# Softmax exponentials head by head on ScalarE, with the maximum as bias and the sum as a by-product

## The reference, cut to what matters

```
h = max(layernorm(x), 0)
x = x + L0(h, adj, adj, b)            # A = adj h, C = adj h + b; maximum over nodes of relu
h = max(layernorm(x), 0)              # (of layer 1)
q, k, v = h Wq + bq, h Wk + bk, h Wv + bv        # 8 heads of 64
scores  = q k^T / 8 + (adj == 0 ? -1e9 : 0)
weights = softmax(scores)             # over the keys, for each head and row
out     = x + weights v
```

## Time and profile before

| what | value |
|---|---|
| time, median of 3 runs | 1316.65 us (1316.41 to 1317.42) |
| the profiled execution's own time | 1314.74 us |
| its span, first to last instruction | 1313.0 us |
| TensorE busy | 1283.2 us, 98% |
| VectorE busy | 1056.3 us, 80% |
| ScalarE busy | 945.6 us, 72% |
| GpSimd busy | 1028.8 us, 78% |
| granted TensorE clock, mean | 0.994 of full |

### The profile page before, as it was taken

How to read it: one execution, slowest core, us unless ns; L and a number is a source line. 1 busy time by engine, 2 the same in 40 slices (tenths; PEclk the granted TensorE clock), 3 DMA queues, 4 the chain that set the end, 5 groups by cost and what they waited for, 6 DMA issues and landing times.

```text
span 1313.0 us, 30866 instructions
## 1 busy us (share of the span) xinstructions
PE 1283.2 (98%) x11193; PEld 670.7 (51%) x11193; DVE 1056.3 (80%) x2217; ACT 945.6 (72%) x1451; POOL 1028.8 (78%) x1165
## 2 busy tenths in 40 slices
PE   6999999999999999999999999999999999999995
PEld 3455555555555555555555555555555555555553
DVE  7588788788788888888888888887887887888777
ACT  6877777777777777777777777777777777777665
POOL 5887877887887888788788778778778778878665
PEclk9999999999999999999999999999999999999998
DMA  6366566566555555555555655655665665664344
GB/s 201 67 137 137 123 143 133 127 138 136 130 132 142 131 124 145 135 121 146 137 122 138 139 127 134 137 133 127 139 137 121 141 142 121 136 144 116 89 89 112
DMA packets 435237, 171.68 MB, mean 131 GB/s; under 512 B 400528, under 2 KB 400656, under 8 KB 435088
## 3 DMA queue, kind: packets, MB, share of 16 engines
q1 hardware_dynamic: 433744, 169.46, 56.2%
q10 hardware_dynamic: 1344, 0.27, 0.1%
HBM read 37.03 MB, written 33.55 MB: 54 GB/s over the span
## 4 chain that ended last, share of the span: by engine, by line
PE 94%; DVE 3%; ACT 1%; issue 1%; POOL 0%; DMA 0%; POOLq 0%; DVEq 0%; ACTq 0%
PE proj L892 50%; PE proj L910 24%; PE sc L928 7%; PE proj L951 7%; PE proj L875 6%; DVE shifted L634 0%; DVE w L744 0%; DVE masked L622 0%; DVE row_max L626 0%; DMA x_in<-in_x 0%; ACT qk L442 0%; POOL probs L343 0%; DVE q_peaks L756 0%; ACT h L429 0%; ACT qkT L440 0%
## 5 line engine op out<-in xcount | busy, mean ns | idle before, releaser
L892 PE MATMUL proj<-hT,w 128*128 128x512 f16 x3072 | 706.1, 380 | 2.3 <-DVE hT L796 2.0
L892 PEld LDWEIGHTS proj<-hT,w 128*128 128x128 f16 x3072 | 295.6, 98 | 357.3 <-issue 3.6
L336 POOL TENSOR_TENSOR qkT<-qk,qkT 128x512 f16<-128x512 f32 x256 | 315.7, 1233 | 66.9 <-ACT qk L442 66.4
L910 PE MATMUL proj<-w,hT 128*128 128x512 f16 x1536 | 352.2, 379 | 0.4 <-DVE v L611 0.3
L343 POOL TENSOR_TENSOR probs<-probs 128x1024 f16<-128x1024 f32 x127 | 271.2, 2136 | 21.7 <-ACT probs L460 21.5
L458 ACT ACTIVATE probs<-shifted 128x1024 f16<-128x1024 f32 x127 | 134.3, 1057 | 181.3 <-DVE shifted L634 181.2
L440 ACT ACTIVATE qkT<-proj,bqk_up 128x512 f16<-128x512 f32 x256 | 173.5, 678 | 102.7 <-PE proj L892 102.7
L611 DVE SCALAR_TENSOR_TENSOR v<-proj,v 128x512 f16<-128x512 f32 x128 | 88.4, 691 | 162.9 <-ACT v L448 162.9
L910 PEld LDWEIGHTS proj<-w,hT 128*128 128x128 f16 x1536 | 141.6, 98 | 152.4 <-DVE v L611 0.7
L634 DVE TENSOR_TENSOR shifted<-masked,row_max 128x1024 f32<-128x1024 f32 x127 | 207.7, 1635 | 2.3
L656 DVE SCALAR_TENSOR_TENSOR y<-proj,out_scale,x 128x64 f32<-128x64 f32 x992 | 201.7, 277 | 4.6 <-DVE out_scale L645 0.3
(11 more groups left out here) (84 smaller groups left out, 1023.5 us busy)
## 6 DMA issues: line engine op xcount, KB each, us to landing
x_in<-in_x SPq DMA_DIRECT2D x128, 256.0 KB, 3.0
out_x<-y SPq DMA_DIRECT2D x128, 256.0 KB, 2.4
probsT<-probs SPq DMA_TRANSPOSE x127, 3.7
hT<-h SPq DMA_TRANSPOSE x124, 3.1
w_raw<-in_L_gnn_Wq SPq DMA_DIRECT2D x4, 256.0 KB, 7.4
w_raw<-in_L_gnn_Wk SPq DMA_DIRECT2D x1, 1024.0 KB, 9.3
w_raw<-in_L_gnn_Wv SPq DMA_DIRECT2D x1, 1024.0 KB, 11.6
bv_rows<-in_L_gnn_bv ACTq DMA_DIRECT2D x1, 256.0 KB, 7.2
```

Of the source, the lines that this page charges most:

```text
L336: pool.tensor_tensor(qk_place(k, u, 1), qk32[:, u % 2, :], qk_place(k, u, 0), ALU.subtract).then_inc(qk_rest_done, 1)
L892: last = nc.tensor.matmul(proj[:, QK_BANKS[u % 2], :], w16[:, j, s, c, col * P:(col + 1) * P], hT[:, k // GROUP % HT_GROUPS, t, c, :, :].r ...
L910: last = nc.tensor.matmul(v_bank(m), hT[:, m // GROUP % HT_GROUPS, s, c, k % GROUP, :], w16[:, 2, t, c, :], start=(c == 0 and i == 0), sto ...
```

## The change

VectorE no longer makes `shifted`. It makes `minus_max`, the row maximum times -1/8, 8 columns. ScalarE takes the exponentials straight from `masked`, with 1/8 as scale and `minus_max` as bias; since a bias is one value per row and each head has its own, a wide instruction becomes eight of 128 columns, one per head, in both copies. The float copy also adds up its row (`accum_out`) into `sums`. `masked` gets a second buffer, with a wait for the exponentials of two graphs before. v loses its column of ones, a graph's output fits one bank, and TensorE's two waits for the shared bank go. VectorE takes `scaled_sum` from `sums` after the exponentials instead of from TensorE's product, and waits for that product only in front of the eight y instructions. The tail is changed in the same way. The core of the diff:

```diff
-                    act.wait_ge(shifted_done, m + 1)
+                    act.wait_ge(minus_max_done, m + 1)
                     wait(act, probsT_done[k % 2], (m - k % 2) * 8)
-                    nc.scalar.activation(probs16[:, k % 2, 0, :, :], shifted[:, :, :], ACT.Exp, scale=HD ** -0.5).then_inc(probs_head_done, 1)
+                    for h in range(H):
+                        last = nc.scalar.activation(probs16[:, k % 2, 0, h, :], masked[:, k % 2, h, :], ACT.Exp,
+                                                    scale=HD ** -0.5, bias=minus_max[:, k % 2, h:h + 1])
+                    last.then_inc(probs_head_done, 1)
                     wait(act, probs_rest_done, m)
-                    nc.scalar.activation(probs[:, :, :], shifted[:, :, :], ACT.Exp, scale=HD ** -0.5).then_inc(probs_done, 1)
+                    wait(act, sum_done, m - GROUP + 1)
+                    for h in range(H):
+                        last = nc.scalar.activation(probs[:, h, :], masked[:, k % 2, h, :], ACT.Exp, scale=HD ** -0.5,
+                                                    bias=minus_max[:, k % 2, h:h + 1], accum_out=sums[:, k % GROUP, h:h + 1])
+                    last.then_inc(probs_done, 1)
...
-                    wait(dve, shifted_done, m)
+                    wait(dve, minus_max_done, m)
+                    wait(dve, probs_done, m - 1)
                     dve.wait_ge(s_ready, m + 1)
...
                     dve.wait_ge(max_done, m + 1)
-                    wait(dve, probs_done, m)
-                    nc.vector.tensor_tensor(shifted[:, :, :], masked[:, :, :],
-                                            row_max[:, :].unsqueeze(2).to_broadcast([P, H, P]), ALU.subtract).then_inc(shifted_done, 1)
+                    nc.vector.tensor_scalar(minus_max[:, k % 2, :], row_max[:, :], -HD ** -0.5, None, ALU.mult).then_inc(minus_max_done, 1)
...
-                dve.wait_ge(o_ready, m + 1)
-                nc.vector.tensor_scalar(scaled_sum[:, :, :], o_view(m)[:, :, :, HD], redo[:, 2:3], None,
-                                        ALU.mult).then_inc(sum_done, 1)
+                dve.wait_ge(probs_done, m + 1)
+                nc.vector.tensor_scalar(scaled_sum[:, :], sums[:, m % GROUP, :], redo[:, 2:3], None, ALU.mult).then_inc(sum_done, 1)
...
                     dve.wait_ge(out_scale_done, count or m + 1)
+                    dve.wait_ge(o_ready, m + 1)
                     dve.wait_ge(x1_done, m + 1)
...
-                    if u % 2 == 0:
-                        wait(pe, y_low_done, base + k - Y_BEHIND)
...
-                    wait(pe, qk_evac, min(2 * (m + OUT_BEHIND) + 1, 2 * B))
...
-                            w = HD if t else VW
-                            last = nc.tensor.matmul(o_view(m)[:, h % 2, h // 2, 0:w], probsT[:, k % 2, s, h % 2 * 4 + h // 2, :],
-                                                    v16[:, t, k % GROUP, h, 0:w],
+                            last = nc.tensor.matmul(o_head(m, h), probsT[:, k % 2, s, place(h), :],
+                                                    v16[:, t, k % GROUP, h, :],
                                                     start=(i == 0), stop=(i == 2))
```

More of the change, by code:

```diff
@@ L93, in graph_layers @@
         qkT = sb("qkT", [P, 2, 2, 2, KC, GROUP, P], F16)
-        v16 = sb("v16", [P, 2, GROUP, H, VP], F16)
-        masked = sb("masked", [P, H, P])
+        v16 = sb("v16", [P, 2, GROUP, H, HD], F16)
+        masked = sb("masked", [P, 2, H, P])
         row_max = sb("row_max", [P, H])
-        shifted = sb("shifted", [P, H, P])
+        minus_max = sb("minus_max", [P, 2, H])
         probs = sb("probs", [P, H, P])
@@ L100, in graph_layers @@
         probsT = sb("probsT", [P, 2, 2, H, P], F16)
-        scaled_sum = sb("scaled_sum", [P, 2, H // 2])
-        out_scale = sb("out_scale", [P, 2, 2, H // 2])
+        sums = sb("sums", [P, GROUP, H])
+        scaled_sum = sb("scaled_sum", [P, H])
+        out_scale = sb("out_scale", [P, GROUP, H])
         proj = ps("proj", [P, 4, 512])
@@ L188, in score_banks, with place, o_head, scale_of @@
             return sc[:, 2 * (m % 2):2 * (m % 2) + 2, :]
-        def o_view(m):
-            return o_late if m == B - 4 else o_last if m == B - 1 else o_low
+        def place(h):
+            return h % 2 * HALF + h // 2
+        def o_head(m, h):
+            if m == B - 1:
+                return sc[:, 2 + h % 2, h // 2 * HD:h // 2 * HD + HD]
+            bank = sc[:, 0, :] if m == B - 4 else proj[:, O_HIGH, :]
+            return bank[:, place(h) * HD:place(h) * HD + HD]
+        def scale_of(m, h):
+            return out_scale[:, m % GROUP, place(h):place(h) + 1]
         def group_T(k):
@@ L551, in last_exps @@
                 heads = last_heads(half)
-                act.wait_ge(shifted_done, B + half)
+                act.wait_ge(minus_max_done, B + half)
                 act.wait_ge(probsT_done[1], (B - 2) * 8)
-                nc.scalar.activation(probs16[:, 1, 0, heads, :], shifted[:, heads, :], ACT.Exp, scale=HD ** -0.5).then_inc(probs_head_done, 1)
+                for h in range(H // 2 * half, H // 2 * half + H // 2):
+                    last = nc.scalar.activation(probs16[:, 1, 0, h, :], masked[:, 1, h, :], ACT.Exp,
+                                                scale=HD ** -0.5, bias=minus_max[:, 1, h:h + 1])
+                last.then_inc(probs_head_done, 1)
                 act.wait_ge(probs_rest_done, B - 1)
-                nc.scalar.activation(probs[:, heads, :], shifted[:, heads, :], ACT.Exp, scale=HD ** -0.5).then_inc(probs_done, 1)
+                act.wait_ge(sum_done, B - GROUP)
+                for h in range(H // 2 * half, H // 2 * half + H // 2):
+                    last = nc.scalar.activation(probs[:, h, :], masked[:, 1, h, :], ACT.Exp, scale=HD ** -0.5,
+                                                bias=minus_max[:, 1, h:h + 1], accum_out=sums[:, (B - 1) % GROUP, h:h + 1])
+                last.then_inc(probs_done, 1)
             def last_probsT(half):
@@ L625, in softmax_masked @@
                     dve.wait_ge(masked_done, m + 1)
-                    nc.vector.tensor_reduce(row_max[:, :], masked[:, :, :], AX.X, ALU.max).then_inc(max_done, 1)
+                    nc.vector.tensor_reduce(row_max[:, :], masked[:, k % 2, :, :], AX.X, ALU.max).then_inc(max_done, 1)
             def softmax_shift(base, k):
@@ L665, in last_softmax @@
                 heads = last_heads(half)
-                wait(dve, shifted_done, B - 1)
+                wait(dve, minus_max_done, B - 1)
+                dve.wait_ge(probs_done, B - 2)
                 dve.wait_ge(s_ready, B)
-                nc.vector.scalar_tensor_tensor(masked[:, heads, :], score_banks(B - 1)[:, half, :].rearrange("p (h n) -> p h n", n=P),
+                nc.vector.scalar_tensor_tensor(masked[:, 1, heads, :], score_banks(B - 1)[:, half, :].rearrange("p (h n) -> p h n", n=P),
                                                score_scale[:, :], mask8[:, :].unsqueeze(1).to_broadcast([P, H // 2, P]),
@@ L671, in last_softmax @@
                 dve.wait_ge(masked_done, B + half)
-                nc.vector.tensor_reduce(row_max[:, heads], masked[:, heads, :], AX.X, ALU.max).then_inc(max_done, 1)
+                nc.vector.tensor_reduce(row_max[:, heads], masked[:, 1, heads, :], AX.X, ALU.max).then_inc(max_done, 1)
                 dve.wait_ge(max_done, B + half)
-                dve.wait_ge(probs_done, B - 1)
-                nc.vector.tensor_tensor(shifted[:, heads, :], masked[:, heads, :],
-                                        row_max[:, heads].unsqueeze(2).to_broadcast([P, H // 2, P]), ALU.subtract).then_inc(shifted_done, 1)
+                nc.vector.tensor_scalar(minus_max[:, 1, heads], row_max[:, heads], -HD ** -0.5, None, ALU.mult).then_inc(minus_max_done, 1)
@@ L678, in last_out @@
             def last_out(half, count):
                 m = B - 1
-                dve.wait_ge(last_o_ready, half + 1)
[L682 to L686, removed]
+                heads = last_heads(half)
@@ L687, in last_out @@
+                dve.wait_ge(probs_done, B + half)
+                nc.vector.tensor_scalar(scaled_sum[:, heads], sums[:, (B - 1) % GROUP, heads], redo[:, 2:3], None, ALU.mult).then_inc(sum_done, 1)
+                dve.wait_ge(sum_done, count)
+                nc.vector.reciprocal(out_scale[:, (B - 1) % GROUP, heads], scaled_sum[:, heads]).then_inc(out_scale_done, 1)
+                dve.wait_ge(out_scale_done, count)
+                dve.wait_ge(last_o_ready, half + 1)
                 dve.wait_ge(x1_done, B)
@@ L688, in last_out @@
                 dve.wait_ge(y_stored[m % Y_RING], 16 * (m // Y_RING))
[L689 to L692, removed]
+                for h in range(half, H, 2):
+                    cols = slice(h * HD, h * HD + HD)
+                    last = nc.vector.scalar_tensor_tensor(y[:, m % Y_RING, cols], o_head(m, h), scale_of(m, h),
@@ L1018, in last_probs_times_v @@
                     for i, (s, t) in enumerate(PAIRS):
```

(5 more changed lines are left out.)

33 lines of the change are left out of this document (13 added, 20 removed).

## The result

The kernel after takes 1566.12 us (median of four runs, 1565.57 to 1567.18); the kernel before, on the same chip, 1316.53 us (1316.25 to 1317.42). The ratio is 1.189, interval 1.188 to 1.191. The forecast was 1535 us in a range of 1418 to 1720: right in its sign, inside the range, 31 us low. The profiled execution is the run of 1565.57 us, with a span of 1563.8 us.

A forecast was written before the change was run, and what follows sets the result against it. TensorE, 94% of the span, was taken to bound the kernel before; after the change, a loop through ScalarE and VectorE. 1314.74 us + 208 (123 slots) + 10 (end of run) = 1533, stated as 1535 us; range 1418 to 1720.

The forecast's parts named there:

- The loop: From ScalarE's v through VectorE's masking, maximum, minus_max to exponentials, two qk, x, next v: 11.62 us a slot, +208 us.
- Exponentials: On ScalarE, sixteen 128-column exponentials with pointer bias a slot: 0.30 us each, bounds 0.254 to 0.315, sums priced separately.
- Sums: On ScalarE, eight of the exponentials a slot also add up their row: 0.10 us each for the read-out.
- rival 2: Each sum's read-out on ScalarE costs like a small ACTIVATE, 0.28 us: 184 us more, 1719 us; chance 0.20.
- rival 3: The sum in ScalarE's exponentials is free: 102 us less, 1433 us; chance 0.12.
- The failed term: minus_max on VectorE, 8 columns, priced at 0.20 us like the 8-column reciprocal; 0 or twice that would move 25 us.
- Signs: Profile after: ScalarE above 90% busy, TensorE near 85%, ScalarE waiting about 1 us a slot, TensorE idle before adjacency product.
- Rival 4: VectorE gets ahead, the loop doesn't bind, ScalarE runs without pause at 10.67 us a slot: 1418 us; chance 0.07.
- Rival 5: Not slower: the sixteen exponentials, sums included, stay under 3.9 us, TensorE sets the slot: 1315 to 1316 us; chance 0.06.
- Tail: End of the run on ScalarE, from the exponentials on: 35.1 us instead of 24.3, about +10 us.
- Ones column: On TensorE, 16 of a slot's 24 probability products stream 64 columns for 65: 0.01 us saved.

The follow-up runs named there:

- The changed order with the fold: Kernel after, VectorE's masking and maximum put ahead of the rest of v, minus_max folded into the masked scores: 1428.41 us, ratio 1.085 to the kernel before.
- third one-pass form: Kernel after with only float exponentials on ScalarE, VectorE converting them to half precision ahead of y, minus_max folded into the masked scores: 1332.95 us, ratio 1.012.

## Why the prediction was right, and what was mis-sized

- **What binds.** The loop was named whole, and it is what binds: the chain runs through it, and what was taken out of it moved the time by nearly its full amount: 0.094 us for each sum, and for minus_max 103 us of the 112 that the loop gave.
- **Exponentials.** 0.30 each was forecast and 0.294 measured. The estimate between x less its columns and the wide row plus a pointer held; its parts too, 0.09 for the pointer (0.294 against 0.201) and, for one without, 0.225 against 0.201.
- **Sums.** 0.10 forecast, 0.093 measured. The Trainium skill's rule in "VectorE: DVE Perf Modes", section "Two Vector instructions with no wait between them", that an op which writes its accumulator out is two instructions, holds on ScalarE as well: the second is a row of its own. It costs a third of c's 0.28, so rival 2's 1719 was too high and rival 3's 1433 too low. Together the sixteen cost 5.43 us for 5.6.
- **The failed term.** "The nearest row is the 8-column reciprocal, 0.20 us" priced minus_max. It measured 0.31 in odd slots and 0.95 in even ones. From v to the exponentials it was 4.14 and 5.25 us instead of 4.03 and 4.51: +0.425 in the mean, less 0.17 for the cheaper exponentials, is +0.255, and times 123 that is the 31 us. My bound for it, twice 0.20, was also too tight: I took the length of the row and did not ask what GpSimd does at that moment. The old profile has a tensor_scalar of eight columns too, scaled_sum, 0.21 us in the mean; in the pair of slots that I read it had beside it only GpSimd instructions of 0.2 to 0.6 us. Late in the run, though, it also ran beside a long one, and did not wait for it:
```profile
1231.85 2.13 POOL L343 TENSOR_TENSOR probs<-probs 128x1024 f16<-128x1024 f32 x1 [1.17 <-ACT probs L460]
1232.05 0.23 DVE L642 TENSOR_SCALAR scaled_sum<-proj,redo 128x8 f32<-128x8 f32 x1 [1.78 <-PE proj L951]
```
It read its eight columns out of PSUM there, every 65th column of `proj`; minus_max reads eight neighbouring columns out of SBUF, as scaled_sum does in the kernel after, where it ran 1.18 us in the tail, until 0.03 us after GpSimd. So the kind of instruction alone does not make it wait, and that old row could not have shown the wait. Which of the two differences decides, no run separates.
- **Signs.** TensorE at 85%, the wait for minus_max (1.3 us a slot, 1 forecast) and the idle time in front of the adjacency product came as written; ScalarE stood at 88%, not above 90, since its exponentials were cheaper and its waits longer than forecast.
- **Rivals 4 and 5.** Rival 4 needed VectorE ahead of ScalarE, which it is not in the kernel after. The changed order with the fold brings it about; there a slot in which ScalarE is not held up is 10.49 us (forecast 10.67), and the time 1428 (forecast 1418). Rival 5 needed the sixteen under 3.9 us, sums included; they take 5.43. Only without pointers and sums are they below it, at 3.22, and then the shift is still in the loop.
- **Tail.** 34.5 us for 35.1.
- **Ones column.** 0.03 us a slot for 0.01, too little to matter; why it is more than the column's share of the stream is open. My description of its place in PSUM was wrong: four heads at 65 columns are 260 of the 512 columns of a bank, about half; it is eight, 520 columns, that don't fit one bank.

## What to carry to other kernels

An engine with 27% of idle time is not free if a loop through another engine runs over it: add the pieces from one start to the next around the loop before counting slack. A wide instruction that is cut into one per head pays its fixed cost, pointer and read-out each time; here 1.92 us became 5.43. Before a short VectorE instruction goes into a tight path, look at what GpSimd does beside it, and see whether a sign or a factor can be folded into an instruction that is there anyway.

## What the runs showed of the hardware

- An ACTIVATE with a sum leaves a second instruction behind it, ACTIVATION_READ_ACCUMULATOR, 188 ns long in the mean, which delays the next start by 93 ns.
- A pointer bias costs an ACTIVATE of 128 columns 0.09 us (0.294 against 0.201 from start to start).
- A tensor_scalar of eight neighbouring SBUF columns on VectorE ran until the GpSimd instruction beside it had ended, up to 1.05 us in the slots of the kernel after, 1.18 in its tail and 1.72 in the third one-pass form; a reduction of the same size took 0.15 us beside the same instruction, and a tensor_scalar of eight columns out of PSUM 0.23 us beside one of 2.13.
